# Fewer visits to the turns, another engine for the last copies, and one feature of seven tiles fetched row by row from SyncE

## The chip, the cores and the metric

The kernel runs on one core of one Trainium2 chip. The core has TensorE (PE: matmuls, and "turns", matmuls against an identity that transpose a block), VectorE (DVE), ScalarE (ACT), GpSimd (POOL) and SyncE (SP). Here POOL issues the indirect transfers that gather rows, and SP issues all other transfers. The metric is the device time in microseconds (us) of one execution; the time of a kernel is the median of several. A change is told from no change when it exceeds about 0.2% of the time, some 1.15 us.

## The reference

The kernel is a recommender tower for 2048 samples. Each has 27 ids; id f picks a row of 128 floats from table f. The layer input is the 27 rows side by side (3456 values), the 351 products of each pair of rows, and 16 dense values. Three layers follow.

```python
e = jnp.stack([tbl_0[ids[:, 0]], ..., tbl_26[ids[:, 26]]], axis=1)      # 2048 x 27 x 128
interactions = jnp.einsum('bfd,bgd->bfg', e, e)                          # pair products
flat_interactions = interactions[:, _TRIU_I, _TRIU_J]                    # 351 of them
h = jnp.concatenate([e.reshape(B, -1), flat_interactions, dense_ctx], axis=1)   # 2048 x 3823
h = jnp.maximum(h @ W_top1 + b_top1, 0.0)                                # 512
h = jnp.maximum(h @ W_top2 + b_top2, 0.0)                                # 256
y = h @ W_top3                                                           # 1
```

## The kernel before, in words

The samples are cut into 16 tiles of 128. The 27 features of a tile are cut into 7 groups (`GROUPS`: six of 4 features, the last of 3), called g0 to g6. Feature 23 is the last one of g5. (15, g2) means group 2 of tile 15. Every engine runs its own list of instructions in the order in which the code writes them; semaphores hold them to each other. Nothing is reordered by a scheduler.

For each tile:

- POOL issues one indirect transfer a feature (line 242), each for 128 rows of 512 bytes, into the buffer `emb`, which has one slot a feature. The gather of a feature of tile t waits only until PE has turned that group of tile t-1.
- PE turns each group (`turn_group`, line 269) into one of two banks of `ps_t`. A turn of group n waits for the gathers of the group and for the copy of group n-2.
- ACT rounds the turned group to the "high" part (`split_group`, line 534), then DVE takes what is left as the "low" part (line 645). Both go to `emb_x`.
- PE multiplies each feature by the weights of layer 1 in three matmuls of 512 columns (`multiply`, lines 298 to 300), so a group of 4 has 12 of them.
- PE makes the pair products in 16 "gram units" of two matmuls each (`gram_unit`, line 323), numbered k = 0 to 15, in three banks. ACT copies out the even units and DVE the odd ones (`take_blocks`, lines 582 and 666), four copies a unit. The features whose multiplies are not done yet are spread between the units by the table `BEFORE_UNIT`.
- DVE turns the pair products in blocks (line 680), adds and packs them (lines 687, 702). PE turns the packed columns (`turn_columns`, line 352), ACT copies them, and PE multiplies them (`multiply_columns`, line 356). Then follow the activation, its turn (`turn_h1`, line 393) and layer 2 (`layer_2`, line 400), all one tile late.

In the order of PE a tile looks like this (t > 0): multiply g0, turn g2, multiply g1, turn g3, multiply g2, turn g4, multiply g3, turn the columns, turn g5, multiply two features, multiply the columns, turn g6, then the 16 gram units with the other nine features between them. After unit 8 stand the turns of h1 and of (t+1, g0), after unit 14 those of (t+1, g1), after unit 15 layer 2. A "visit" below is a run of turns with nothing else between; there are seven visits to turns a tile. The last tile has an order of its own, in which the turn of feature 26 (line 286) stands alone and last, since its gather is the last of all.

SP loads the weights of layer 1 in 27 pieces during tile 0, some later weights and constants, and then waits for the last tile to store the output.

## Time and profile before

| | |
|---|---|
| time, median of 3 runs | 574.94 us (574.45 to 575.32) |
| the profiled execution: its time | 576.18 us |
| the profiled execution: its span, first to last instruction | 574.4 us |
| mean granted clock of PE in it | 0.991 |
| busy: PE / its weight loads / DVE / ACT / POOL | 93% / 83% / 60% / 41% / 73% |

The profile shows one execution. Busy shares are averages over the span and say nothing of who waits for whom; PE's matmuls overlap, so 93% is not PE at its peak. The time beside the span, 1.8 us, lies outside the first and last instruction. Starts of rows are in us from the first instruction.

### The profile page before, as it was taken

The page shows a single profiled execution, that of the slowest core. Times are in us where ns is not written, and L with a number is a line of the kernel's source. Part 1 is how long each engine was busy: PE and PEld are TensorE (multiplying, and loading weights), DVE is VectorE, ACT ScalarE, POOL GpSimd, SP SyncE. Part 2 cuts the span into 40 slices and gives each one's busy share as a digit, 9 for nine tenths or more (in the row PEclk, how much of TensorE's full clock was granted, in tenths as well). Part 3 has the DMA queues.
Part 4 walks back from the last instruction along what each step waited for, and adds up shares of the span by engine and source line. Part 5 has one row for each costly group of instructions (what it writes and reads, how often), then busy time and mean ns, then how long its engine had stood idle before and what let it go on. Part 6 is the DMA issues. An engine that isn't in the chain of part 4 may idle for free.

```text
span 574.4 us, 7882 instructions
## 1 busy us (share of the span) xinstructions
PE 535.3 (93%) x2578; PEld 478.4 (83%) x2578; DVE 347.4 (60%) x1140; ACT 233.3 (41%) x703; POOL 417.9 (73%) x450
## 2 busy tenths in 40 slices
PE   0786999999999999999999999999999999999998
PEld 0775988888998888889888898988889888889875
DVE  2756638375583837658373665837467483746754
ACT  3646144351614426262442625335261533517151
POOL 6777777777777777777777777777777777777711
PEclk9989899999999999999999999999999999999999
DMA  7756111211212222121212121212112121212100
GB/s 236 247 161 170 52 53 52 55 51 51 56 51 56 52 55 52 53 54 50 57 51 56 51 55 51 55 53 54 53 51 56 51 57 51 55 51 56 51 15 2
DMA packets 19582, 37.84 MB, mean 66 GB/s; under 512 B 7781, under 2 KB 8805, under 8 KB 19541
## 3 DMA queue, kind: packets, MB, share of 16 engines
q0 software_dynamic: 13824, 28.34, 18.6%
q1 hardware_dynamic: 5716, 8.99, 4.9%
q8 instruction: 21, 0.34, 0.2%
q14 instruction: 21, 0.16, 0.1%
HBM read 37.30 MB, written 0.01 MB: 65 GB/s over the span
## 4 chain that ended last, share of the span: by engine, by line
POOL 69%; issue 22%; PE 6%; DMA 1%; ACT 1%; DVE 0%; ACTq 0%; POOLq 0%; DVEq 0%
POOL emb L242 69%; PE ps_acc L298 1%; PE ps_acc L356 1%; DMA emb<-in_tbl,idx 1%; PE ps_acc L299 1%; PE ps_acc L300 1%; PE ps_gram L323 1%; ACT g_buf L591 0%; PE ps_t L435 0%; PE ps_t L269 0%; DMA idx_first<-in_ids 0%; PE ps_acc L408 0%; PE ps_gram L345 0%; PE ps_t L345 0%; PE ps_t L427 0%
## 5 line engine op out<-in xcount | busy, mean ns | idle before, releaser
L242 POOL DMA_INDIRECT emb<-in_tbl,idx x405 | 386.4, 954 | 123.4 <-issue 121.0
L298 PE MATMUL ps_acc<-w_hi,emb_x 128*128 128x512 f32 x432 | 200.6, 464 | 5.8 <-DVE emb_x L645 5.8
L299 PE MATMUL ps_acc<-w_lo,emb_x 128*128 128x512 f32 x432 | 174.4, 404 | 0.0
L300 PE MATMUL ps_acc<-w_hi,emb_x 128*128 128x512 f32 x432 | 173.4, 401 | 0.0
L645 DVE TENSOR_TENSOR emb_x<-ps_t,emb_x 128x512 fp32r<-128x512 f32 (+1 forms) x111 | 74.1, 667 | 152.5 <-ACT emb_x L534 152.1
L666 DVE COPY g_buf<-ps_gram 32x112 f32<-32x112 f32 x480 | 129.6, 270 | 55.9 <-PE ps_gram L323 49.8
L534 ACT ACTIVATE emb_x<-ps_t 128x512 fp32r<-128x512 f32 (+1 forms) x111 | 63.2, 583 | 223.8 <-PE ps_t L269 223.4
L582 ACT ACTIVATE g_buf<-ps_gram 32x112 f32<-32x112 f32 x480 | 122.6, 255 | 51.9 <-PE ps_gram L323 46.5
L298 PEld LDWEIGHTS ps_acc<-w_hi,emb_x 128*128 128x128 f32 x432 | 131.1, 303 | 11.5 <-issue 8.8
L299 PEld LDWEIGHTS ps_acc<-w_lo,emb_x 128*128 128x128 f32 x432 | 134.5, 311 | 0.6
L300 PEld LDWEIGHTS ps_acc<-w_hi,emb_x 128*128 128x128 f32 x432 | 131.8, 305 | 0.8
L269 PE MATMUL ps_t<-ident,emb 128*128 128x128 f32 x429 | 67.9, 281 | 27.5 <-DMA emb<-in_tbl,idx_first 18.9
L269 PEld LDWEIGHTS ps_t<-ident,emb 128*128 128x128 f32 x429 | 51.8, 143 | 44.9 <-issue 20.7
L323 PEld LDWEIGHTS ps_gram<-emb_x 128*128 128x128 f32 x480 | 69.2, 189 | 11.1 <-ACT g_buf L582 4.2
L323 PE MATMUL ps_gram<-emb_x 128*128 128x224 f32 x480 | 75.3, 285 | 2.1 <-DVE g_buf L666 1.2
L680 DVE STREAM_TRANSPOSE g_buf<-g_buf 128x1792 f32<-128x1792 f32 x16 | 59.0, 3686 | 0.1
L356 PE MATMUL ps_acc<-w_cols,cols_t 128*128 128x512 f32 (+1 forms) x96 | 44.0, 593 | 0.1
L702 DVE TENSOR_TENSOR cols<-gram,g_buf 128x26 f32<-128x26 f32 (+25 forms) x406 | 39.1, 173 | 0.0
L242 POOL DMA_INDIRECT emb<-in_tbl,idx_first x27 | 28.0, 1035 | 9.3 <-issue 7.9
L356 PEld LDWEIGHTS ps_acc<-w_cols,cols_t 128*128 128x128 f32 (+1 forms) x96 | 18.0, 190 | 16.1 <-issue 14.7
L400 PE MATMUL ps_gram<-w,h_t 128*128 128x256 f32 x112 | 26.5, 380 | 0.0
L400 PEld LDWEIGHTS ps_gram<-w,h_t 128*128 128x128 f32 x112 | 20.2, 190 | 2.2
(61 smaller groups left out, 162.8 us busy)
## 6 DMA issues: line engine op xcount, KB each, us to landing
g_buf<-in_W_top SPq DMA_DIRECT2D x27, 256.0 KB, 4.2
emb<-in_tbl,idx POOLq DMA_INDIRECT x405, 2.5
w_cols<-in_W_top SPq DMA_DIRECT2D x1, 512.0 KB
w<-in_W_top SPq DMA_DIRECT2D x1, 512.0 KB
emb<-in_tbl,idx_first POOLq DMA_INDIRECT x27, 3.9
w_cols<-in_W_top SPq DMA_DIRECT2D x1, 222.0 KB
idx<-in_ids SPq DMA_DIRECT2D x1, 216.0 KB, 5.4
ctx_rows<-in_dense_ctx SPq DMA_DIRECT2D x4, 32.0 KB, 5.3
```

The costliest lines, as they stand in the source:

```text
L242: pool.indirect_dma_start(out=emb[:, f * D:(f + 1) * D], out_offset=None, in_=tables[f], in_offset=bass.IndirectOffsetOnAxis(ap=rows, axis ...
L269: last = pe.transpose(turned_bank(n, g)[:, :, i], emb[:, f * D:(f + 1) * D], ident[:, :])
L298: pe.matmul(acc, emb_part(0, f), w_hi[:, f, :], start=(f == 0), stop=False)
L299: pe.matmul(acc, emb_part(0, f), w_lo[:, f, :], start=False, stop=False)
L300: last = pe.matmul(acc, emb_part(1, f), w_hi[:, f, :], start=False, stop=False)
L323: last = pe.matmul(ps_gram[:, n % BANKS, i * NJ * XW:(i + 1) * NJ * XW], gram_weights(q), gram_stream(q), start=True, stop=True)
L356: return pe.matmul(ps_acc[:, t % 2, :], cols_t[0:k, n * P:(n + 1) * P], w_cols[0:k, n, :], start=False, stop=(n == NCC - 1))
L534: act.activation(group_part(0, g), turned_bank(n, g), ACT.Copy).then_inc(s_emb_hi, 1)
L582: last = act.activation(target, source, ACT.Copy)
L645: dve.tensor_tensor(group_part(1, g), turned_bank(n, g), group_part(0, g).bitcast(fp32), ALU.subtract).then_inc(s_emb_lo, 1)
L666: last = dve.tensor_copy(target, source)
L680: dve.transpose(g_turned.rearrange("p n f -> p (n f)"), g_raw.rearrange("p q n -> p n q")).then_inc(s_turned, 1)
```

## The change

There are three parts.

**The order of a tile.** PE turns g2 and g3 in one visit, g4, g5 and the columns in one, g6 alone, and h1, (t+1, g0) and (t+1, g1) in one after unit 11. The table `BEFORE_UNIT` now spreads eleven features instead of nine. ACT and DVE follow: ACT splits (t+1, g0) ahead of its last gram unit, DVE splits it after its last one, the columns are taken after g5, and DVE packs them in one go after g3.

**Who copies the last two gram units.** Unit 14 goes from ACT to DVE and unit 15 from DVE to ACT.

**Feature 23 of tiles 3, 5, 7, 9, 11, 13 and 15.** POOL leaves these seven gathers out. SP loads the ids of these 7 x 128 rows to a small buffer with seven transfers, reads them into registers 32 at a time, and issues one transfer of one row (512 bytes) for each, 896 in all, into a buffer `ahead` of its own that holds all seven tiles. PE's turn of g5 in these tiles waits for the 128 rows as well (`s_ahead`).

```diff
+    ACT_UNITS = [k for k in range(UNITS - 2) if k % 2 == 0] + [UNITS - 1]
+    DVE_UNITS = [k for k in range(UNITS - 2) if k % 2 == 1] + [UNITS - 2]
...
+    AHEAD = 23
+    AHEAD_TILES = [3, 5, 7, 9, 11, 13, 15]
+    LOAD = 32
...
@@ SP, after the weights' loads
+                for n, t in enumerate(AHEAD_TILES):
+                    sp.dma_start(idx_ahead[n:n + 1, :], ids.rearrange(
+                        "(p t) f -> t f p", t=TILES)[t, AHEAD:AHEAD + 1, :]
+                        ).then_inc(s_ids_ahead, 16)
             sp.wait_ge(s_pe_t, NG)
...
+            sp.wait_ge(s_ids_ahead, 16 * NA)
+            for n in range(NA):
+                for p in range(0, P, LOAD):
+                    _, picked = nc.values_load_multi_w_load_instructions(
+                        idx_ahead[n:n + 1, p:p + LOAD], engines=[mybir.EngineType.SP],
...
+                    for i in range(LOAD):
+                        sp.dma_start(ahead[p + i:p + i + 1, n, :],
+                                     tables[AHEAD][bass.ds(picked[i], 1), :]
+                                     ).then_inc(s_ahead[n], 16)
             sp.wait_ge(s_y, TILES)
@@ POOL
                     for f in GROUPS[g]:
+                        if fetched_ahead(t, f):
+                            continue
@@ PE, turn_group
-                pe.wait_ge(s_gather[g], (t + 1) * 16 * len(GROUPS[g]))
+                pe.wait_ge(s_gather[g], gathered(t, g))
+                if AHEAD in GROUPS[g] and t in AHEAD_TILES:
+                    pe.wait_ge(s_ahead[AHEAD_TILES.index(t)], 16 * P)
@@ PE, the tiles
-            BEFORE_UNIT = [2, 0, 0, 2, 0, 0, 2, 0, 0, 1, 0, 0, 2, 0, 0, 0]
+            BEFORE_UNIT = [2, 0, 0, 2, 0, 0, 2, 0, 0, 2, 0, 0, 1, 0, 2, 0]
...
                 turn_group(t, 2)
+                turn_group(t, 3)
                 multiply_group(t, 1)
-                turn_group(t, 3)
                 multiply_group(t, 2)
                 turn_group(t, 4)
-                multiply_group(t, 3)
+                turn_group(t, 5)
                 if t > 0:
                     turn_columns(t - 1)
-                turn_group(t, 5)
-                f = 4 * GF
-                for _ in range(GF if t == 0 else 2):
-                    multiply(t, f)
-                    f += 1
+                multiply_group(t, 3)
                 if t > 0:
                     multiply_columns(t - 1)
                 turn_group(t, 6)
...
-                    if k == 8 and t > 0:
-                        turn_h1(t - 1)
-                    if k in (8, 14):
-                        turn_group(t + 1, (k - 8) // 6)
+                    if k == 11:
+                        if t > 0:
+                            turn_h1(t - 1)
+                        turn_group(t + 1, 0)
+                        turn_group(t + 1, 1)
@@ ACT, the tiles
-                for k in range(0, UNITS, 2):
+                for k in ACT_UNITS:
+                    if k == UNITS - 1:
+                        split_group(t + 1, 0)
                     take_blocks(t, k)
-                    if t > 0 and k == 8:
+                    if t > 0 and k == 10:
                         take_h1(t - 1)
@@ DVE, the tiles
-                for k in range(1, UNITS, 2):
-                    if k == UNITS - 1:
-                        split_group(t + 1, 0)
+                for k in DVE_UNITS:
                     take_blocks(t, k)
+                split_group(t + 1, 0)
                 split_group(t + 1, 1)
```

The rows that follow show how the built programs stand. In the changed program the same helpers have other line numbers: `turn_group` 315, `multiply` 344 to 346, `gram_unit` 369, `turn_columns` 398, `layer_2` 446; the square brackets name the semaphores that a row waits for.

PE before, in the middle of a tile: the end of the multiplies of g3, the columns (352), g5 (269), then features 16 and 17.

```order
L298 MATMUL ps_acc<-w_hi,emb_x 128x512
L299 MATMUL ps_acc<-w_lo,emb_x 128x512
L300 MATMUL ps_acc<-w_hi,emb_x 128x512
L352 MATMUL ps_gram<-ident,cols 128x4x32 [waits s_h2,s_cols]
L352 MATMUL ps_gram<-ident,cols 128x4x32
L352 MATMUL ps_gram<-ident,cols 112x4x32
L269 MATMUL ps_t<-ident,emb 128x128 [waits s_emb_lo,s_gather5]
L269 MATMUL ps_t<-ident,emb 128x128 x3
L298 MATMUL ps_acc<-w_hi,emb_x 128x512 [waits s_emb_lo]
L299 MATMUL ps_acc<-w_lo,emb_x 128x512
L300 MATMUL ps_acc<-w_hi,emb_x 128x512
```

PE in the changed program, the same place: the end of the multiplies of g2, then g4, g5 and the columns in one visit, then the multiplies of g3.

```order
L346 MATMUL ps_acc<-w_hi,emb_x 128x512
L315 MATMUL ps_t<-ident,emb 128x128 [waits s_emb_lo,s_gather4]
L315 MATMUL ps_t<-ident,emb 128x128 x3
L315 MATMUL ps_t<-ident,emb 128x128 [waits s_emb_lo,s_gather5]
L315 MATMUL ps_t<-ident,emb 128x128 x3
L398 MATMUL ps_gram<-ident,cols 128x4x32 [waits s_h2,s_cols]
L398 MATMUL ps_gram<-ident,cols 128x4x32
L398 MATMUL ps_gram<-ident,cols 112x4x32
L344 MATMUL ps_acc<-w_hi,emb_x 128x512 [waits s_emb_lo]
L345 MATMUL ps_acc<-w_lo,emb_x 128x512
L346 MATMUL ps_acc<-w_hi,emb_x 128x512
```

The turn of g5 now stands ahead of the 12 matmuls of g3, and it has one return to multiplies with g4 and the columns instead of two.

PE before, at the end of a tile: unit 14, the turns of (t+1, g1), unit 15, layer 2 (400), and the first multiply of the next tile.

```order
L323 MATMUL ps_gram<-emb_x 128x224 [waits s_dve_raw]
L323 MATMUL ps_gram<-emb_x 128x224
L269 MATMUL ps_t<-ident,emb 128x128 [waits s_emb_lo,s_gather1]
L269 MATMUL ps_t<-ident,emb 128x128 x3
L323 MATMUL ps_gram<-emb_x 128x224 [waits s_act_raw]
L323 MATMUL ps_gram<-emb_x 128x224
L400 MATMUL ps_gram<-w,h_t 128x256 [waits s_h1_out]
L400 MATMUL ps_gram<-w,h_t 128x256 x3
L298 MATMUL ps_acc<-w_hi,emb_x 128x512 [waits s_emb_lo,s_h1]
```

PE in the changed program, the same place: the last multiply ahead of unit 14, units 14 and 15, layer 2, the next tile.

```order
L346 MATMUL ps_acc<-w_hi,emb_x 128x512
L369 MATMUL ps_gram<-emb_x 128x224 [waits s_dve_raw]
L369 MATMUL ps_gram<-emb_x 128x224
L369 MATMUL ps_gram<-emb_x 128x224 [waits s_act_raw]
L369 MATMUL ps_gram<-emb_x 128x224
L446 MATMUL ps_gram<-w,h_t 128x256 [waits s_h1_out]
L446 MATMUL ps_gram<-w,h_t 128x256 x3
L344 MATMUL ps_acc<-w_hi,emb_x 128x512 [waits s_emb_lo,s_h1]
```

The turns of (t+1, g1) no longer stand between units 14 and 15; they went up to the visit after unit 11, and two multiplies stand ahead of unit 14 instead.

SP before, its last rows, then SP in the changed program from the same place on.

```order
L213 DMA ctx_rows<-in_dense_ctx 32x256 x4
L215 DMA b_rows<-in_b_top 128x256
L216 DMA w_rows<-in_W_top 128x256
L220 DMA out<-y 128x16 [waits s_y]
L55 UNCONDITIONAL_BRANCH [waits s_stored]
```

```order
L244 DMA ctx_rows<-in_dense_ctx 32x256 x4
L246 DMA b_rows<-in_b_top 128x256
L247 DMA w_rows<-in_W_top 128x256
L253 TENSOR_LOAD idx_ahead [waits s_ids_ahead]
L258 ISA
L258 DMA ahead<-in_tbl 1x128
L258 ISA
L258 DMA ahead<-in_tbl 1x128
L258 ISA
L258 DMA ahead<-in_tbl 1x128
```

Each row fetched costs SP one register instruction (ISA, it makes the address from the id) and one transfer; a load of 32 ids (TENSOR_LOAD) stands ahead of every 32 rows. The store of the output is now queued behind all 896 rows.

## Rows read from the trace of the kernel before

**Rows 1.** The page: the chain that ended last, by engine.

```profile
POOL 69%; issue 22%; PE 6%; DMA 1%; ACT 1%; DVE 0%; ACTq 0%; POOLq 0%; DVEq 0%
```

**Rows 2.** The page: gathers; count, busy us, mean ns, idle before, its cause.

```profile
L242 POOL DMA_INDIRECT emb<-in_tbl,idx x405 | 386.4, 954 | 123.4 <-issue 121.0
```

**Rows 3.** Timeline of POOL: start, us, instruction, idle before; end of (14, g5), last gather.

```profile
509.36 0.94 POOL L242 DMA_INDIRECT emb<-in_tbl,idx  x1 [0.30 <-issue]
...
547.60 0.94 POOL L242 DMA_INDIRECT emb<-in_tbl,idx  x1 [0.30 <-issue]
```

**Rows 4.** Timeline of PE: the turn of g5 in tiles 1, 2 and 14.

```profile
72.78 0.60 PE L269 MATMUL ps_t<-ident,emb 128*128 128x128 f32 x4
...
105.90 0.60 PE L269 MATMUL ps_t<-ident,emb 128*128 128x128 f32 x4
...
511.85 0.66 PE L269 MATMUL ps_t<-ident,emb 128*128 128x128 f32 x4 [0.49 <-DMA emb<-in_tbl,idx]
```

**Rows 5.** Timeline of PE: from multiplies to a visit and back.

```profile
267.04 0.39 PE L300 MATMUL ps_acc<-w_hi,emb_x 128*128 128x512 f32 x1
267.27 0.60 PE L269 MATMUL ps_t<-ident,emb 128*128 128x128 f32 x4
267.63 0.58 PE L298 MATMUL ps_acc<-w_hi,emb_x 128*128 128x512 f32 x1
268.05 0.40 PE L299 MATMUL ps_acc<-w_lo,emb_x 128*128 128x512 f32 x1
```

**Rows 6.** Timeline of PE: from gram units to multiplies, and the end of a tile.

```profile
248.28 0.52 PE L298 MATMUL ps_acc<-w_hi,emb_x 128*128 128x512 f32 x1
248.64 0.40 PE L299 MATMUL ps_acc<-w_lo,emb_x 128*128 128x512 f32 x1
...
257.65 0.60 PE L269 MATMUL ps_t<-ident,emb 128*128 128x128 f32 x4
258.30 0.49 PE L323 MATMUL ps_gram<-emb_x 128*128 128x224 f32 x2
258.62 1.90 PE L400 MATMUL ps_gram<-w,h_t 128*128 128x256 f32 x8
260.82 0.58 PE L298 MATMUL ps_acc<-w_hi,emb_x 128*128 128x512 f32 x1 [0.30 <-DVE emb_x L645]
```

**Rows 7.** Timeline of DVE: the split of (t+1, g0) and the last copies of a tile.

```profile
259.99 0.69 DVE L645 TENSOR_TENSOR emb_x<-ps_t,emb_x 128x512 fp32r<-128x512 f32 x1 [1.45 <-ACT emb_x L534]
260.59 1.11 DVE L666 COPY g_buf<-ps_gram 32x112 f32<-32x112 f32 x4
```

**Rows 8.** Timeline of PE: turns of tile 15 (g2, g3, g4, columns, g5, 24-25, 26).

```profile
531.48 0.63 PE L269 MATMUL ps_t<-ident,emb 128*128 128x128 f32 x4 [0.31 <-DVE emb_x L645]
...
536.29 0.60 PE L269 MATMUL ps_t<-ident,emb 128*128 128x128 f32 x4
...
541.36 0.66 PE L269 MATMUL ps_t<-ident,emb 128*128 128x128 f32 x4
...
541.96 0.30 PEld L352 LDWEIGHTS ps_gram<-ident,cols 128*128 128x128 f32 x3 [0.19 <-DVE cols L702]
...
546.45 0.65 PE L269 MATMUL ps_t<-ident,emb 128*128 128x128 f32 x4
...
548.98 0.44 PE L279 MATMUL ps_t<-ident,emb 128*128 128x128 f32 x2
550.20 0.33 PE L286 MATMUL ps_t<-ident,emb 128*128 128x128 f32 x1 [0.79 <-DMA emb<-in_tbl,idx]
```

**Rows 9.** Timeline of SP: issues; the first is for a single partition, the last for 128..

```profile
41.81 0.28 SPq L206 DMA_DIRECT2D w_cols<-in_b_top  x1
42.13 0.54 SPq L208 DMA_DIRECT2D w<-in_W_top  x1
...
45.21 0.43 SPq L216 DMA_DIRECT2D w_rows<-in_W_top  x1
```

**Rows 10.** Windows of all engines: busy us, granted clock, DMA share, GB/s.

```profile
240.00:274.00 34.00, 33.12 (x163) 29.84 (x163) 20.80 (x71) 13.74 (x43) 25.77 (x28) 1.00 0.20 53
```

More of the change, by code:

```diff
@@ L73, in dlrm_tower_kernel @@
         emb = sb("emb", [P, NF * D])
+        ahead = sb("ahead", [P, NA, D])
+        idx_ahead = sb("idx_ahead", [NA, P], i32)
         g_buf = sb("g_buf", [P, 2 * Q * XW])
@@ L109, in dlrm_tower_kernel @@
         s_gather_last = sem("s_gather_last")
+        s_ids_ahead = sem("s_ids_ahead")
+        s_ahead = [sem(f"s_ahead{t}") for t in AHEAD_TILES]
         s_zero = sem("s_zero")
@@ L138, in dlrm_tower_kernel, with fetched_ahead, rows_of, gathered @@
         s_stored = sem("s_stored")
+        def fetched_ahead(t, f):
+            return f == AHEAD and t in AHEAD_TILES
+        def rows_of(t, f):
+            if fetched_ahead(t, f):
+                return ahead[:, AHEAD_TILES.index(t), :]
+            return emb[:, f * D:(f + 1) * D]
+        def gathered(t, g):
+            return 16 * sum(1 for u in range(t + 1) for f in GROUPS[g] if not fetched_ahead(u, f))
         def emb_part(part, f):
@@ L198, in _ @@
                                  ids.rearrange("(p t) f -> p (t f)", t=TILES)).then_inc(s_ids, 16)
+            with nc.allow_non_contiguous_dma(reason="one id of every row of ids"):
+                for n, t in enumerate(AHEAD_TILES):
+                    sp.dma_start(idx_ahead[n:n + 1, :], ids.rearrange(
+                        "(p t) f -> t f p", t=TILES)[t, AHEAD:AHEAD + 1, :]
+                        ).then_inc(s_ids_ahead, 16)
             sp.wait_ge(s_pe_t, NG)
@@ L218, in _ @@
                          ).then_inc(s_const, 16)
+            sp.wait_ge(s_ids_ahead, 16 * NA)
[3 more added lines that the diff above has]
+                        idx_ahead[n:n + 1, p:p + LOAD], engines=[mybir.EngineType.SP],
+                        min_val=0, max_val=tables[AHEAD].shape[0] - 1,
+                        skip_runtime_bounds_check_because="an id is a row of its table")
+                    for i in range(LOAD):
+                        sp.dma_start(ahead[p + i:p + i + 1, n, :],
+                                     tables[AHEAD][bass.ds(picked[i], 1), :]
+                                     ).then_inc(s_ahead[n], 16)
             sp.wait_ge(s_y, TILES)
@@ L237, in _ @@
                     for f in GROUPS[g]:
+                        if fetched_ahead(t, f):
+                            continue
                         landed = s_gather[g]
@@ L268, in turn_group @@
                 for i, f in enumerate(GROUPS[g]):
-                    last = pe.transpose(turned_bank(n, g)[:, :, i], emb[:, f * D:(f + 1) * D],
+                    last = pe.transpose(turned_bank(n, g)[:, :, i], rows_of(t, f),
                                         ident[:, :])
@@ L278, in turn_last_group @@
                 for i, f in enumerate(GROUPS[g][:-1]):
-                    last = pe.transpose(turned_bank(n, g)[:, :, i], emb[:, f * D:(f + 1) * D],
+                    last = pe.transpose(turned_bank(n, g)[:, :, i], rows_of(t, f),
                                         ident[:, :])
@@ L466, in _ @@
                 turn_group(t, 6)
+                f = 4 * GF
                 for k in range(UNITS):
@@ L610, in _ @@
                             split_weights(c)
-                    split_group(t, g)
-                    if t > 0 and g == 4:
+                    if t == 0 or g > 0:
+                        split_group(t, g)
+                    if t > 0 and g == 5:
                         take_columns(t - 1)
@@ L615, in _ @@
                         relu_h1(t - 1)
-                for k in range(0, UNITS, 2):
+                for k in ACT_UNITS:
+                    if k == UNITS - 1:
+                        split_group(t + 1, 0)
                     take_blocks(t, k)
-                    if t > 0 and k == 8:
+                    if t > 0 and k == 10:
                         take_h1(t - 1)
             t = TILES - 1
-            for g in range(5):
+            for g in range(1, 5):
                 split_group(t, g)
```

18 lines of the change are left out of this document (7 added, 11 removed).

## The prediction

> **What bounds the kernel now.** Read the chain that ended last first: POOL and "issue" make 91% of it [rows 1]. The group of the gathers says why. A gather keeps POOL 0.95 us, and nearly all the idle time between gathers, 121.0 of 123.4 us, is put down to POOL's own issue and not to another engine [rows 2]. POOL runs gather behind gather, 0.94 + 0.30 = 1.25 us each [rows 3], from the start to the last one at 547.60. Next look at PE where it needs what POOL brings. In tile 14 the turn of g5 waits for its gather and starts 2.49 us after POOL started the last one, 509.36 to 511.85 [rows 3, 4]. In tiles 1 and 2 the same turn waits for nothing, and the distance between them, 105.90 - 72.78 = 33.12 us, is what a tile costs PE alone. From tile 2 to 14 it is (511.85 - 105.90)/12 = 33.83 us, POOL's pace of 27 x 1.25 = 33.75 and a little. So two engines are close: POOL 33.8 and PE 33.1 a tile. A gain on one of them alone is worth at most 0.7 us a tile; the change works on both. PE's clock stays at 2.4 GHz in the steady part (1.00 in the window), and the transfers fill a fifth of the DMA engines [rows 10].
>
> **The gathers left out.** Seven of 1.25 us: POOL ends 8.75 us earlier. Six of them lie ahead of (14, g5). Its data come 7.50 us earlier, and its turn can start at 511.85 - 7.50 = 504.35. POOL needs nothing that the change brings later: the gather of a group waits for the turn of one tile before, which is some 20 us old.
>
> **What the new order saves PE in a tile.** A return from turns to multiplies: from the start of four turns to the second matmul behind them are 268.05 - 267.27 = 0.78 us; four turns at 0.11 (the third and fourth of a waiting group add 0.66 - 0.44 = 0.22 to two, rows 8) and one matmul at 0.24 would be 0.68. So a return costs 0.10 [rows 5]. Two such returns go. The visit between units 14 and 15 costs more: 258.30 - 257.65 = 0.65 for four turns (0.44), and 0.32 for the two matmuls behind it (0.22), together 0.31 [rows 6]; it goes. One more return from gram units to multiplies comes: 0.36 instead of 0.24, so 0.12 [rows 6]. Sum: -0.20 - 0.31 + 0.12 = -0.39. At the start of a tile PE idles 0.30 for DVE's low part of g0 [rows 6, 7]. In the new order DVE copies unit 14 (1.11) and then splits g0 (0.60) behind the unit's matmuls; with about 0.3 to start and 0.15 to be seen, 2.2 us. PE meanwhile has unit 15 and layer 2, some 2.1 (the latter 1.90 busy less its tail). I put 0.1 of the wait as left: -0.20. PE alone then needs 33.12 - 0.39 - 0.20 = 32.5 us a tile. The copies move between ACT and DVE one for one, and both have idle time (13.7 and 20.8 of 34 busy [rows 10]): nothing.
>
> **What sets the pace then.** POOL's pair of tiles takes 2 x 33.83 - 1.25, a mean of 33.2 a tile. PE's 32.5 is below it. So POOL still sets the pace and PE's own saving shows as longer waits at g5, not as time, until tile 14.
>
> **The end.** From (14, g5) on PE has more to do than before, since the turn now stands ahead of the multiplies of g3. Before: 531.48 - 511.85 = 19.63 us to the turn of (15, g2) [rows 4, 8]. Added: 12 matmuls at 0.24 = 2.87 and the three turns of the columns, 0.33. Gone: 0.31 of the visit, 0.20 of the wait for DVE. Back: 0.12. Sum 22.44. From (15, g2) to the last turn, L286, were 550.20 - 531.48 = 18.72, the order of the code there is unchanged, but waits are in it that fall away when gathers come early: 0.95 at L286 (1.22 from the turn of features 24 and 25, which takes 0.27), 0.23 at (15, g4) (5.07 from g3 for four turns and six features that make 4.84), and 0.19 at the columns [rows 8]. Left 17.35. The last turn comes at 504.35 + 22.44 + 17.35 = 544.14. Its gather alone would allow 550.20 - 8.75 = 541.45, so PE sets it: the last tile and a half are PE's. Behind L286 nothing is changed: 574.4 - 550.20 = 24.2. End of the span 568.3, that is 6.1 less. Against the profiled execution's own time, 576.18, that is 570.1; the median of the runs is 1.24 below that execution, so **568.8**.
>
> **SP's rows.** 896 times a register instruction and a transfer, and 28 loads of ids. The trace has no such transfer. Nearest is the one to a single partition, 42.13 - 41.81 = 0.32 from its start to the next; one over 128 partitions lasts 0.43 [rows 9]. For the register instruction I know no row; it should lie between nothing and a whole issue, 0.28. A load of ids for 32 rows costs at most what a gather takes to land, 2.49, so 0.08 a row. Bounds: 0.32 and 0.68 us a row. I take 0.45, near the row for one partition. The loop starts when the last constant is issued, 45.6, and its first ids are there, 48.1. The rows of tile 3 are due at about 138: (138 - 50.6)/128 = 0.68. The last are due at the turn of (15, g5), 544.14 - 3.75 + 0.95 = 541.3: (541.3 - 2.5 - 48.1)/896 = **0.548 us a row**. Below it the rows cost nothing, all under POOL's and PE's time. The edge lies inside my bounds. Behind PE's wait for them stands all of PE's list, and behind that POOL's next gathers; behind SP's rows stands only the store.
>
> The Trainium skill, "DMA: Bandwidth & Descriptors", section "Latency and other measured facts", puts the floor of a tensor load at about 0.6 us; by it the loads would be 0.02 a row instead of 0.08, and the rate 0.4. No row here shows one.
>
> **Rivals.**
> - *SP is too slow.* For: no row for the register instruction, and 896 issues in a row where before there were 40. Against: the single-partition issue, 0.32, leaves 0.23 for the rest. It decides from 0.548 us a row; no gain is left at 0.554. At 0.60 the last rows are issued at 48.1 + 537.6, land 2.5 later, and 574.4 - 546.45 = 28.0 follow: 616.2, median 616.7. Slower.
> - *Rows land one by one.* A one-row transfer may end before the next starts to move. Then a row takes what a gather takes from issue to use, 2.49 [rows 3, 4]: 50.6 + 896 x 2.49 + 28 = 2310 us. Against: gathers start every 1.25 and take 2.49, so they overlap. The page's section "Anatomy of one DMA" has a fixed cost of about 2 us in each, and its rules for kernel authors call small transfers mostly overhead; the trace agrees on the size of it, and shows that it overlaps.
> - *The rows disturb the gathers.* They share DMA engines that are 0.20 busy [rows 10]. If each gather grew by 0.01 us, some 365 of them ahead of (14, g5) shift it by 3.6: 572.5. Against: the rows are 0.46 MB in 490 us, 1 GB/s beside 53. The page's section on a DMA's semaphore says a transfer of few parts uses the lowest-numbered engines; then all rows sit on one engine, with one sixteenth of each gather, which speaks for this rival. No row here shows it.
> - *The long visits make PE wait.* Two groups in a visit need both banks free and DVE's packing done ahead of the columns. If a tile costs PE 33.8, PE sets the pace from tile 1 on: (1, g5) at 72.78 [rows 4] less up to 3 because it stands earlier in the tile, say 71, 13 tiles of 33.8, then 22.44 + 17.35 + 24.2 = 64.0 to the end: 574.4, median 574.9, the same. It starts to cost at 33.2, that is 0.7 us of new waits a tile.
> - *All of POOL's 8.75 show.* If PE loses 2.7 less in the last tile and a half: 566.2.
>
> **How the numbers follow.** Forecast 0.60, with a range of its own of 567.0 to 570.5; SP too slow 0.15; one by one 0.02; disturbed gathers 0.12; long visits 0.06; all of POOL's gain 0.05. Within 0.2% of 574.94 is 573.8 to 576.1, what a measurement can't tell from no change. Faster: 0.60 + 0.05 + 0.10 + 0.02 = 0.77; the same 0.06; slower 0.17. The range, 565.8 to 575.0, takes in all but the two on SP and part of the long visits, about 0.2.
>
> **What would show it.** POOL: 398 gathers by idx, still 1.25 apart, the last one starting near 538.9. PE: waits for gathers at g5 of about 1.5 us in even tiles and a few tenths in odd ones, no wait for a gather at L286; a turn of (15, g2) 5 us earlier than 531.48. SP: rows less than 0.548 apart, done before 541. The forecast is wrong if g5 of odd tiles waits for `ahead`, if the gathers' spacing grows, or if PE's tiles in which it waits for nothing take over 33 us.

## The result, and the profile after

The changed kernel takes 569.41 us, median of 4 runs (568.90 to 569.92); the kernel before 575.13 (574.45 to 575.85, 4 runs, three of them those of the table of before). The ratio is 0.990, interval 0.9883 to 0.9918: faster by 5.7 us, where 6.1 was forecast. The profiled execution took 569.48 and spans 567.6; 568.3 was forecast for the span.

The chain that ended last, from the page, answers to [rows 1]: PE has taken POOL's place as its largest part.

```profile
PE 55%; POOL 29%; issue 10%; DMA 5%; ACT 1%; DVE 1%; ACTq 0%; POOLq 0%; DVEq 0%
```

The group of the gathers (count, busy us, mean ns, idle before, its cause) answers to [rows 2]: seven are gone, the mean of one is what it was.

```profile
L286 POOL DMA_INDIRECT emb<-in_tbl,idx x398 | 379.3, 953 | 121.4 <-issue 116.3
```

POOL's timeline answers to [rows 3]: the last gather of (14, g5), and the last of all, 9.3 us earlier than before.

```profile
501.36 0.95 POOL L286 DMA_INDIRECT emb<-in_tbl,idx  x1 [0.30 <-issue]
...
538.30 0.95 POOL L286 DMA_INDIRECT emb<-in_tbl,idx  x1 [0.30 <-issue]
```

PE's timeline answers to [rows 4, 8]: the visit of g4 and g5 in tiles 2 and 3, then the turns of (14, g5), (15, g2) and the last one, and the first gram pair of the last feature behind it.

```profile
105.63 1.04 PE L315 MATMUL ps_t<-ident,emb 128*128 128x128 f32 x8
...
137.83 0.93 PE L315 MATMUL ps_t<-ident,emb 128*128 128x128 f32 x7
138.59 0.27 PE L315 MATMUL ps_t<-ident,ahead 128*128 128x128 f32 x1
...
503.92 0.66 PE L315 MATMUL ps_t<-ident,emb 128*128 128x128 f32 x4 [1.46 <-DMA emb<-in_tbl,idx]
...
526.03 0.41 PE L315 MATMUL ps_t<-ident,emb 128*128 128x128 f32 x2
...
543.21 0.27 PE L332 MATMUL ps_t<-ident,emb 128*128 128x128 f32 x1
...
544.64 1.15 PE L391 MATMUL ps_gram<-emb_x 128*128 128x224 f32 x8 [0.36 <-DVE emb_x L700]
```

Two tiles without a wait stand 137.83 - 105.63 = 32.2 us apart (33.12 before). From tile 6 on PE waits for gathers at g5 as forecast: 1.4 to 1.7 us in the even tiles, 0.2 to 0.7 in tiles 7, 9 and 11, nothing in 13. At (14, g5) it still waits 1.46. At the last turn it waits for nothing: its gather was started 4.9 us earlier, where 2.5 to 2.6 are needed.

SP answers to [rows 9]. By instruction (duration in ns, min/median/max; first and last start in us): the loads of 32 ids, the transfers of the ids, and the three instructions of a row.

```profile
L253 SPq TENSOR_LOAD <-idx_ahead x28: 2072/2126/2193, 46.2 to 465.1; - x28
L229 SPq DMA_DIRECT2D idx_ahead<-in_ids x7: 592/597/630, 36.8 to 40.7; - x7
```

```profile
L258 SPq FUSED_REGOPS  x896: 37/37/51, 48.3 to 480.0; - x180
L258 SPq MOVE ahead<-in_tbl x896: 29/29/42, 48.4 to 480.0; - x180
L258 SPq DMA_DIRECT2D ahead<-in_tbl x896: 224/225/314, 48.5 to 480.1; - x180
```

The 896 rows take 480.1 - 48.5 = 431.6 us, 0.482 a row. A row without its load is 0.42 of it ((431.6 - 27 x 2.13)/895), the load 0.067. The last row is issued 60 us ahead of its turn.

### The profile page after: what moved, and what is told of

It reads as the page before. It is cut to its first block, busy times and chain, and to the rows that moved or that the text cites. A ratio compares the mean times of both kernels' runs of the same rounds, so it can differ in the third digit from the quotient of the medians.

```text
span 567.6 us, 10600 instructions
## 1 busy us (share of the span) xinstructions
PE 527.5 (93%) x2578; PEld 478.9 (84%) x2578; DVE 348.8 (61%) x1140; ACT 230.5 (41%) x703; POOL 410.7 (72%) x443
## 4 chain that ended last, share of the span: by engine, by line
PE 55%; POOL 29%; issue 10%; DMA 5%; ACT 1%; DVE 1%; ACTq 0%; POOLq 0%; DVEq 0%
POOL emb L286 29%; PE ps_acc L344 12%; PE ps_acc L345 10%; PE ps_acc L346 10%; PE ps_gram L369 6%; PE ps_acc L402 5%; PE ps_t L315 5%; DMA emb<-in_tbl,idx 4%; PE ps_gram L446 2%; PE ps_gram L439 1%; PE ps_gram L398 1%; ACT g_buf L632 0%; PE ps_t L481 0%; PE ps_acc L454 0%; DMA idx_first<-in_ids 0%
## 5 line engine op out<-in xcount | busy, mean ns | idle before, releaser
L286 POOL DMA_INDIRECT emb<-in_tbl,idx x398 | 379.3, 953 | 121.4 <-issue 116.3
L689 DVE TENSOR_TENSOR emb_x<-ps_t,emb_x 128x512 fp32r<-128x512 f32 (+1 forms) x111 | 72.6, 668 | 125.6 <-ACT emb_x L575 124.7
L315 PE MATMUL ps_t<-ident,emb 128*128 128x128 f32 x422 | 62.2, 281 | 34.2 <-DMA emb<-in_tbl,idx_first 21.5
L315 PEld LDWEIGHTS ps_t<-ident,emb 128*128 128x128 f32 x422 | 50.5, 144 | 49.6 <-issue 21.2
L369 PEld LDWEIGHTS ps_gram<-emb_x 128*128 128x128 f32 x480 | 70.4, 192 | 4.3
L369 PE MATMUL ps_gram<-emb_x 128*128 128x224 f32 x480 | 71.2, 280 | 0.0
```

What stands on the lines that cost most here:

```text
L286: pool.indirect_dma_start(out=emb[:, f * D:(f + 1) * D], out_offset=None, in_=tables[f], in_offset=bass.IndirectOffsetOnAxis(ap=rows, axis ...
L315: last = pe.transpose(turned_bank(n, g)[:, :, i], rows_of(t, f), ident[:, :])
L369: last = pe.matmul(ps_gram[:, n % BANKS, i * NJ * XW:(i + 1) * NJ * XW], gram_weights(q), gram_stream(q), start=True, stop=True)
L689: dve.tensor_tensor(group_part(1, g), turned_bank(n, g), group_part(0, g).bitcast(fp32), ALU.subtract).then_inc(s_emb_lo, 1)
```

## The experiments

Each kernel was timed in five rounds beside the kernel before, whose medians in the three sets were 575.19 (e1, e2, e5, e6), 575.32 (e3, e4, e7, e8) and 575.44 us (e9 to e12). The interval is that of the ratio to it; kernels of different sets are best compared by their ratios. "Turn" is the first instruction of the turns named; times inside a run come from its one profiled execution, and executions of one kernel differ by 1 us and more (the spans of e7_split_add: 565.2 to 569.1). A "stretched" gather is one that lasts longer than the 0.945 us of most.

**e1_order_only: the new order and engines, all gathers on POOL.**

```diff
-    AHEAD_TILES = [3, 5, 7, 9, 11, 13, 15]
+    AHEAD_TILES = []
```

> The changed kernel without the rows from SyncE: GpSimd gathers all 432 features, everything else as changed. Theory (GpSimd sets the pace up to tile 14, then TensorE's order): the turn of (14, g5) starts again near 511.8; 22.11 us to (15, g2) and 17.18 to the last turn, as in the changed kernel, make 551.1, and 24.4 to the end: span 575.5, 1.1 us longer than before, ratio about 1.002. Waits for gathers at g5 of about 1.6 us in every tile. Rival (the fewer visits bring the gain): each tile gives 0.4 to 0.9 us, the span is 562 to 569.

Measured: 576.65 us, ratio 1.0023 (1.0009 to 1.0037), span 574.6. The turn of (14, g5) starts at 510.98 behind a wait for its gather, the last turn at 550.27.

```profile
510.98 0.33 PE L316 MATMUL ps_t<-ident,emb 128*128 128x128 f32 x1 [1.47 <-DMA emb<-in_tbl,idx]
...
550.27 0.27 PE L333 MATMUL ps_t<-ident,emb 128*128 128x128 f32 x1
```

As expected: PE's saving of 0.9 us a tile goes into waits of 1.3 to 1.5 us at g5 in tiles 3 to 14, and the way from (14, g5) to the last turn is 39.29 us instead of 38.35 [rows 4, 8]. Alone, the order makes the kernel slightly slower: 1.5 us by the medians, 0.2 by the profiled spans.

**e2_rows_only: the rows from SP, order and engines as before.** The edit to the kernel before is the part of the diff on SP, POOL and `turn_group`.

> The kernel before with the 896 rows from SyncE in place of the same seven gathers, and with its old order of visits and old engines for the copies. Theory: GpSimd brings (14, g5) at 503.9, TensorE alone needs 33.12 us a tile and is at that turn at 105.9 + 12 x 33.12 = 503.3, so it is there in time; then 19.6 to (15, g2) and 17.35 to the last turn make 540.9, and its gather allows 540.8: span 565.3, about 2.3 us shorter than the changed kernel, ratio to before about 0.984. Rival (the new order is needed to turn the saved gathers into time): TensorE's 33.12 with new waits of 0.3 or more a tile, span 569 to 573, longer than the changed kernel.

Measured: 570.57 us, ratio 0.9924 (0.9912 to 0.9937), span 568.5: 3.2 us above the expectation. The turn of (14, g5) starts at 506.80 instead of 503.9. Behind it all went about as expected: the last turn is 37.26 later (36.95 expected).

```profile
506.80 0.44 PE L312 MATMUL ps_t<-ident,emb 128*128 128x128 f32 x2 [0.63 <-DMA emb<-in_tbl,idx]
...
544.06 0.27 PE L329 MATMUL ps_t<-ident,emb 128*128 128x128 f32 x1
```

So POOL was late. Most of its gathers last 0.94 to 0.95, but some last up to 1.53. In e2_rows_only (POOL, then DVE, the same stretches):

```profile
364.76 1.43 POOL L283 DMA_INDIRECT emb<-in_tbl,idx  x1 [0.30 <-issue]
...
502.72 1.15 POOL L283 DMA_INDIRECT emb<-in_tbl,idx  x1 [0.31 <-issue]
```

```profile
364.46 0.92 DVE L730 TENSOR_TENSOR gram<-g_buf 128x729 f32<-128x729 f32 x1
...
502.63 0.42 DVE L760 SCALAR_TENSOR_TENSOR h<-h,w_rows 128x256 f32<-128x256 f32 x1
```

The long gather starts 0.30 behind the start of DVE's add of the pair products, ends at 366.19, and the add ends at 365.38: 0.81 earlier. The second one starts 0.09 into an instruction of layer 3 that also reads two SBUF operands (`h`, `w_rows`), and ends 0.82 after it. The changed kernel has the same thing:

```profile
29.52 1.34 POOL L286 DMA_INDIRECT emb<-in_tbl,idx_first  x1 [0.30 <-issue]
...
165.20 0.94 POOL L286 DMA_INDIRECT emb<-in_tbl,idx  x1 [0.30 <-issue]
166.45 1.48 POOL L286 DMA_INDIRECT emb<-in_tbl,idx  x1 [0.30 <-issue]
```

```profile
29.35 0.69 DVE L682 TENSOR_TENSOR w_lo<-g_buf,w_hi 128x512 fp32r<-128x512 f32 x1
...
165.05 0.64 DVE L689 TENSOR_TENSOR emb_x<-ps_t,emb_x 128x512 fp32r<-128x512 f32 x1
166.21 0.91 DVE L731 TENSOR_TENSOR gram<-g_buf 128x729 f32<-128x729 f32 x1
```

A gather that starts inside the add ends some 0.8 us after the add, so one that starts in the add's last 0.1 us loses nothing; nor does one that has started before it (68.85 against an add at 69.12, 0.95). The other rows are a control: the gather at 29.52 starts inside a subtraction of the same size as DVE's splits, but with both operands in SBUF (`g_buf`, `w_hi`: the low part of the weights, only in tile 0), and is stretched; the one at 165.20 starts inside a split, which has one operand in PSUM (`ps_t`), and is not. In all fourteen traces 480 gathers start inside such a split with at least 0.15 us of it left, and none lasts over 0.95.

So the loss is a matter of phase between POOL's 1.25-us beat and the tile, from nothing to 0.7 us a tile. Against a beat of 1.2485 (the spacing of undisturbed gathers from start to start), the gathers of e2_rows_only lose 8.2 us in all, those of the changed kernel 6.2, those of before 6.7. What they lose up to (14, g5), by the DVE instruction that each stretched gather outlasts by 0.8 us:

| us up to (14, g5) | before | e2_rows_only | changed kernel |
|---|---|---|---|
| the weights' low parts, tile 0 | 2.8 | 2.1 | 2.1 |
| the add of the pair products | 1.1 | 3.6 | 1.8 |
| layer 3's instruction (`h`, `w_rows`) | 1.7 | 1.9 | 0 |

Between the last two kernels that is 3.7 us. The last gather of (14, g5) starts 504.18 - 501.36 = 2.8 us later in e2_rows_only. Most of the 0.9 between the two figures is that the undisturbed gathers of the changed kernel's execution last 947 ns each, those of e2_rows_only 944, for which no run shows a cause. The part of the add became the theory of the next kernels.

**e5_late_g5: in tile 14 alone, PE works before it waits.**

```diff
+                late = t == TILES - 2
+                if late:
+                    multiply_group(t, 3)
                 turn_group(t, 5)
                 if t > 0:
                     turn_columns(t - 1)
-                multiply_group(t, 3)
+                if late:
+                    multiply(t, f)
+                    multiply(t, f + 1)
+                    f += 2
+                else:
+                    multiply_group(t, 3)
```

> The changed kernel, but in tile 14 alone the multiplies of g3 stand ahead of the turn of g5 and the columns, and two features of g4 take their place behind it. Theory: TensorE uses the 1.46 us that it waits there. The turn of (14, g5) starts at 505.2 without a wait, four features fewer lie behind it (22.11 - 2.87 = 19.24 to (15, g2)), then 17.18: 541.7 for the last turn, span 566.1, 1.5 us shorter than the changed kernel. Rival (the last tile and a half are held by something else, the copies or GpSimd): no change, 567.6.

Measured: 568.45 us (567.43 to 569.19, 4 runs), ratio 0.9891 (0.9875 to 0.9907), span 565.6, 0.5 below the expectation. The profiled execution is the fastest of the four; by the ratios the kernel and the changed one (0.990) can't be told apart. In the trace the turn needs no wait, and the last turn is 543.21 - 541.27 = 1.9 earlier than in the changed kernel.

```profile
504.07 0.60 PE L315 MATMUL ps_t<-ident,emb 128*128 128x128 f32 x4
...
541.27 0.27 PE L332 MATMUL ps_t<-ident,emb 128*128 128x128 f32 x1
```

The turn starts 0.15 later than in the changed kernel and has 37.20 us behind it instead of 39.29. So from (14, g5) on it is PE's work, not POOL's gathers, that sets the end.

**e6_old_units: the last two units copied by the old engines, the splits of the next g0 behind them.**

```diff
-    ACT_UNITS = [k for k in range(UNITS - 2) if k % 2 == 0] + [UNITS - 1]
-    DVE_UNITS = [k for k in range(UNITS - 2) if k % 2 == 1] + [UNITS - 2]
+    ACT_UNITS = list(range(0, UNITS, 2))
+    DVE_UNITS = list(range(1, UNITS, 2))
...
@@ ACT, the tiles
                 for k in ACT_UNITS:
-                    if k == UNITS - 1:
-                        split_group(t + 1, 0)
                     take_blocks(t, k)
...
+                split_group(t + 1, 0)
```

> The changed kernel with the old engines for the last two gram units: unit 14 by ScalarE, unit 15 by VectorE, the split of the next g0 behind them. Theory: the low part of g0 is ready some 0.7 us later, so TensorE idles about 0.7 us between layer 2 and the next tile; this is hidden behind the gathers up to tile 14, and only the one at the turn of (15, g2) shows: span 567.6 + 0.6 = 568.2. Rival (the swap brings its wait in every tile): 0.7 x 14 more, 577.

Measured: 571.04 us, ratio 0.9934 (0.9921 to 0.9948). Five of the six runs took 569.59 to 571.98 us and one 2831.64, of which nothing here shows the cause; the ratio leaves it out. The profiled execution is the fastest of them, span 567.8, that of the changed kernel within 0.2. A tile now begins with a wait for DVE, and the wait for the gather at (14, g5) is 0.88 instead of 1.46: the one is paid out of the other.

```profile
459.60 0.58 PE L344 MATMUL ps_acc<-w_hi,emb_x 128*128 128x512 f32 x1 [0.62 <-DVE emb_x L688]
...
503.55 0.66 PE L315 MATMUL ps_t<-ident,emb 128*128 128x128 f32 x4 [0.88 <-DMA emb<-in_tbl,idx]
```

From (14, g5) to the last turn it is 39.8 us instead of 39.3, the 0.6 expected. But the interval lies clear above that of the changed kernel (0.9883 to 0.9918), some 2 us: the old engines cost more than the 0.6, and where the rest arises stays open, since the profiled execution doesn't show it.

**e7_split_add: e2_rows_only with DVE's add in three pieces.**

```diff
-                dve.tensor_tensor(gram[:, :, 0:to], g_turned[:, 0:NF, 0:to],
-                                  g_turned[:, GE:GE + NF, 0:to], ALU.add).then_inc(s_sum, 1)
+                cuts = [0, NF] if t == TILES - 1 else [0, 9, 18, NF]
+                for a, b in zip(cuts, cuts[1:]):
+                    last = dve.tensor_tensor(gram[:, a:b, 0:to], g_turned[:, a:b, 0:to],
+                                             g_turned[:, GE + a:GE + b, 0:to], ALU.add)
+                last.then_inc(s_sum, 1)
```

> The kernel of e2_rows_only (rows from SP, old order and old engines of the last units), with DVE's add of the turned pair products (128x729 in one instruction, 0.91 us) cut into three of nine features each, except in the last tile. Theory 1, gathers on POOL are stretched while this add reads two SBUF operands: a gather then lasts at most some 0.2 us too long where it was up to 0.58; of the 8.2 us of excess over a spacing of 1.2485 some 2.5 to 3 go, the turn of (14, g5) starts at 504.3 instead of 506.8, and the span is 566.0 instead of 568.5. Theory 2, the 3.2 us by which e2_rows_only missed have another cause (random, or the new order itself): the excess and the turn stay, span 568.5 plus or minus 0.3.

Measured: 569.48 us (567.48 to 571.32), ratio 0.9890 (0.9859 to 0.9920); profiled span 567.5, turn of (14, g5) at 505.71, loss over the beat 7.5. That is between the two theories: the add's part is 2.0 us up to (14, g5) instead of 3.6, and the size I gave was wrong, since gathers of up to 1.46 us remain. The interval overlaps that of e2_rows_only. POOL, then DVE:

```profile
162.86 1.35 POOL L283 DMA_INDIRECT emb<-in_tbl,idx  x1 [0.31 <-issue]
```

```profile
162.33 1.06 DVE L732 TENSOR_TENSOR gram<-g_buf 128x243 f32<-128x243 f32 x3
```

The pieces stand back to back, the next starts before the last is over, and this gather ends 0.82 after the end of the third. It gets in between pieces only sometimes.

**e8_late_split: e5_late_g5 with the same cut.**

> The kernel of e5_late_g5 with the same add cut into three. Theory 1 (the add stretches gathers): the 1.6 us or so that its stretched gathers cost between 60 and 500 us shrink to 0.5, the turn of (13, g5) and with it all that follows come about 1.0 earlier, span 564.6. Theory 2 (no such effect, or DVE's longer work delays PE): 565.6 or more.

Measured: 569.29 us (568.16 to 570.39), ratio 0.9886 (0.9861 to 0.9911); profiled span 568.3, loss 6.7 where e5_late_g5 had 4.5. Beside the pieces its gathers lose 2.4 us, beside the whole add in e5_late_g5 2.2. No gain here, so cutting the add is no reliable remedy.

**e9_copy: e2_rows_only with the add's second operand taken away.** Half of the sums is left out.

```diff
-                dve.tensor_tensor(gram[:, :, 0:to], g_turned[:, 0:NF, 0:to],
-                                  g_turned[:, GE:GE + NF, 0:to], ALU.add).then_inc(s_sum, 1)
+                dve.tensor_copy(gram[:, :, 0:to], g_turned[:, 0:NF, 0:to]).then_inc(s_sum, 1)
```

> The kernel of e2_rows_only with DVE's add of the pair products (two SBUF operands) replaced by a copy of its first operand, same shape, same target, one SBUF operand; the second half of the sums is left out. Theory 1, it is the second SBUF operand that stretches POOL's gathers: behind the copy no gather lasts over 1.0 us, the 3.7 us of excess from adds go, the turn of (14, g5) starts at 503.5 instead of 506.8, span 565.3. Theory 2, any long DVE instruction of this shape stretches them: excess and turn stay, 568.5. Theory 3, the copy runs in a faster mode that holds the port as well: its row is near 0.5 us instead of 0.91, stretches of up to 0.35 stay, about 567.

Measured: 565.66 us, ratio 0.9827 (0.9801 to 0.9853), 4.9 less than e2_rows_only; span 564.4. The copy lasts as long as the add did, and a gather that starts 0.06 behind its start keeps its 0.94. POOL, then DVE:

```profile
395.54 0.94 POOL L283 DMA_INDIRECT emb<-in_tbl,idx  x1 [0.30 <-issue]
```

```profile
395.48 0.92 DVE L730 COPY gram<-g_buf 128x729 f32<-128x729 f32 x1
```

The groups of the gathers, of e2_rows_only and of e9_copy:

```profile
L283 POOL DMA_INDIRECT emb<-in_tbl,idx x398 | 381.4, 958 | 121.4 <-issue 119.9 <-PE ps_t L312 1.5
```

```profile
L283 POOL DMA_INDIRECT emb<-in_tbl,idx x398 | 376.9, 947 | 121.4 <-issue 117.1 <-PE ps_t L312 4.3
```

4.5 us of POOL are gone: the 3.6 beside the add, as theory 1 has it, and, since the phase is now another, the 1.9 beside layer 3's instruction, less some that came on elsewhere. All fifteen gathers that start around or inside the copy last 0.94 to 0.95. From tile 2 (105.38) to tile 14 the turns of g5 come 33.1 apart, without waiting for gathers: PE's own pace in the old order. The turn of (14, g5), 502.57, no longer waits, and the last turn is at 540.03. The second SBUF operand is shown as the cause: the copy takes it away at the same length, and the splits above, which are two-operand instructions too but with one in PSUM, rule out that it is the kind of operation. (The packing adds behind it have two in SBUF as well: one gather beside them, at 65.11, still lasts 1.32.)

**e10_double_add: the changed kernel with the add done twice.**

```diff
-                dve.tensor_tensor(gram[:, :, 0:to], g_turned[:, 0:NF, 0:to],
-                                  g_turned[:, GE:GE + NF, 0:to], ALU.add).then_inc(s_sum, 1)
+                for out in [gram] if t == TILES - 1 else [again, gram]:
+                    last = dve.tensor_tensor(out[:, :, 0:to], g_turned[:, 0:NF, 0:to],
+                                             g_turned[:, GE:GE + NF, 0:to], ALU.add)
+                last.then_inc(s_sum, 1)
```

> The changed kernel with DVE's add of the pair products done twice in tiles 0 to 14, the first time into a buffer that nobody reads. DVE has the time (it is busy two thirds). Theory 1: a gather in flight ends 0.80 us after the end of the first or the second add, so that some gathers last 1.8 to 2.3 us and the mean loss grows by 0.4 to 0.85 us a tile: the turn of (14, g5) at 509 to 515 instead of 503.9, span 573 to 578. Theory 2, no coupling of DVE's add and POOL: 567.6 plus or minus 0.3, no gather over 1.5 us but where there was one.

Measured: 570.58 us, ratio 0.9915 (0.9892 to 0.9938), span 568.7. The turn of (14, g5) is at 504.16; no gather lasts over 1.54. The size in my theory failed: the gathers beside the two adds lose 4.0 us in all, against 2.1 beside the one of the changed kernel, 0.1 a tile and not 0.4 to 0.85; less lost elsewhere makes the loss over the beat 6.0 against 6.2. POOL, then DVE:

```profile
365.65 1.31 POOL L287 DMA_INDIRECT emb<-in_tbl,idx  x1 [0.31 <-issue]
367.27 0.94 POOL L287 DMA_INDIRECT emb<-in_tbl,idx  x1 [0.30 <-issue]
```

```profile
365.22 0.92 DVE L733 TENSOR_TENSOR again<-g_buf 128x729 f32<-128x729 f32 x1
366.05 0.92 DVE L733 TENSOR_TENSOR gram<-g_buf 128x729 f32<-128x729 f32 x1
```

The gather ends 0.82 behind the end of the first add, and runs while the second one does, which follows at once. Of the extra 1.1 us of span 0.2 are there at (14, g5), and 0.7 is a wait of PE for the columns in the last tile, packed later.

**e3_row14: the rows of tile 14 in place of those of tile 15.**

```diff
-    AHEAD_TILES = [3, 5, 7, 9, 11, 13, 15]
+    AHEAD_TILES = [3, 5, 7, 9, 11, 13, 14]
```

> The changed kernel with feature 23 of tile 14 fetched by SP in place of that of tile 15. If POOL sets the time of the turn of (14, g5) and PE alone what follows: the turn starts 1.25 earlier, 502.7 instead of 503.9, all that follows too, the last gather starts at the same time as before, span 566.35. PE alone from the turn of (13, g5) at 470.0 could be there at 502.2. If PE had set the pace already, the span stays at 567.6. If POOL's last gather set the end, it stays as well.

Measured: 567.64 us (567.04 to 568.43), ratio 0.9861 (0.9837 to 0.9885), span 566.6: the fastest complete kernel of the study. The turn of (14, g5) starts at 502.94, the last at 542.22, both 1.0 earlier though POOL's last gather starts at 538.19 as before. What POOL delivers after (14, g5) doesn't count; what it delivers ahead of it does. (The last gather ahead of it starts 0.9 earlier, not 1.25: those before it ran 0.3 late against the changed kernel's.)

**e4_eight: eight tiles of rows.**

```diff
-    AHEAD_TILES = [3, 5, 7, 9, 11, 13, 15]
+    AHEAD_TILES = [3, 5, 7, 9, 11, 13, 14, 15]
```

> The changed kernel with eight tiles of rows instead of seven (14 as well as 15). SP's rows of 61.66 us a tile from 48.5 on are issued to the end at 541.8 and landed at 543.8. Theory (SP's pace is an edge, and just beyond it PE waits): the turn of feature 23 in (15, g5), which PE could start at 539.35 + 0.3, starts at 543.8; span 543.8 + 27.0 = 570.8, slower than the changed kernel by some 3 us although POOL has one gather less. If the rows' rate is not what limits, it is 566.35 as for e3_row14.

Measured: 576.40 us (574.56 to 577.09, 12 runs), ratio 1.0014 (1.0000 to 1.0029): the whole gain is gone. SP issues its last row at 543.36, and PE waits (the profile names no releaser, "issue"; the semaphore of the rows is what the code waits for there). PE's timeline, then the windows (us, busy of PE, PEld, DVE, ACT, POOL with counts, granted clock, DMA share, GB/s):

```profile
537.58 1.88 PE L402 MATMUL ps_acc<-w_cols,cols_t 128*128 128x512 f32 x4
544.73 0.87 PE L315 MATMUL ps_t<-ident,emb 128*128 128x128 f32 x3 [5.26 <-issue]
...
546.04 0.63 PE L345 MATMUL ps_acc<-w_lo,emb_x 128*128 128x512 f32 x1
546.47 0.63 PE L346 MATMUL ps_acc<-w_hi,emb_x 128*128 128x512 f32 x1
...
549.95 0.40 PE L345 MATMUL ps_acc<-w_lo,emb_x 128*128 128x512 f32 x1
```

```profile
500.00:538.00 38.00, 37.80 (x186) 34.19 (x186) 23.74 (x94) 14.67 (x46) 29.05 (x30) 1.00 0.21 54
538.00:545.00 7.00, 1.74 (x6) 0.69 (x5) 0.00 (x0) 0.60 (x1) 0.47 (x2) 0.85 0.04 13
545.00:549.00 4.00, 4.00 (x14) 3.32 (x13) 0.69 (x1) 0.60 (x1) 0.00 (x0) 0.50 0.00 0
```

The wait was expected. The turn is 0.9 later than forecast: the last row is issued 1.6 later, 0.9 of it because SP's loop began later (49.45), and PE turns 1.4 behind that issue instead of 2.0. Not expected is what follows: behind 5.3 us of idleness PE runs at half its clock, 1.2 GHz, until about 549.9; a matmul takes 0.43 instead of 0.235, start to start. From this turn to the last one take 4.72 us instead of 543.21 - 540.60 = 2.61, so the wait is paid once more in part: 2.1 of the 3.4 us missing from the expectation (570.8 against 574.2), beside the 0.9. Most of the other 0.4 lies behind the last turn, where the granted clock is 0.97 and 0.95 in two windows (1.00 in the changed kernel).

**e11_both: e3_row14 and e5_late_g5 in one.**

> The two edits that shortened the changed kernel in one: the rows of tile 14 instead of tile 15 (e3_row14) and in tile 14 the multiplies of g3 ahead of the turn of g5 and the columns (e5_late_g5). The turn of (14, g5) is PE's own in e5_late_g5, without a wait, so its data 1.25 us earlier bring nothing: if the pace of PE from the turn of (13, g5) sets the end, the last turn is at 541.3 as in e5_late_g5, span 565.6, median 567.6 plus or minus 0.6. If the two gains add up (1.0 and 2.0), span 564.6.

Measured: 568.24 us, ratio 0.9875 (0.9852 to 0.9898), span 566.6. The gains don't add. PE reaches (14, g5) at 504.87 without a wait, where its data would have allowed 502.2 (the last gather starts at 499.67). The last turn is at 542.16, as in e3_row14 (542.22), and the span is the same, 566.6: PE arrives at the turn 1.9 later and has 2.0 less behind it. Once the data are early, turning late brings nothing.

**e12_load16: ids read 16 at a time.**

```diff
-    LOAD = 32
+    LOAD = 16
```

> The changed kernel with the ids read into registers 16 at a time instead of 32, so 56 loads instead of 28. A load of 32 ids takes 2.13 us in the changed kernel's trace. If that price is per load: 70.6 us for the 128 rows of a tile, 0.552 a row; the rows land some 0.5 late for tile 11, 4 late for the turns of g5 in tiles 13 and 15; PE waits there, span 571 to 572. If it is per id: a load takes 1.1 us, the rate stays 0.48 a row, and the span stays 567.6. If between (a floor of 0.6 and the rest per id): 1.35 a load, 0.502 a row, span 567.6 too.

Measured: 570.22 us, ratio 0.9906 (0.9882 to 0.9929), span 568.7. The loads:

```profile
L253 SPq TENSOR_LOAD <-idx_ahead x56: 1134/1232/1402, 47.8 to 485.9; - x56
```

16 ids 1.23 us, 32 ids 2.13: 0.056 an id and 0.34 a load. 0.497 a row, between the two pure cases; no turn of g5 waits for rows. The extra 1.1 us of span are already there at (14, g5), 504.98, where PE waits for a gather: up to there POOL's gathers lose 6.6 over the beat instead of 5.5, and 0.7 of the difference lies in the first 60 us, beside the low parts of the weights.

## Why the prediction was right

*POOL sets the pace until (14, g5).* Right: forecast 504.35, measured 503.92. e1_order_only and e3_row14 show it from two sides: with PE's saving alone nothing is gained; one more gather taken away ahead of (14, g5) brings 1.0, though the last gather of all starts when it did. It isn't the pace in every tile: in tiles 5 and 13 PE waits for no gather.

*PE alone needs 32.5 a tile.* 32.2. The sum of small terms held; the wait of 0.1 that I left at the tile's start isn't there, and the other 0.2 is not traced.

*From (14, g5) to the end PE sets the time.* Right, as e5_late_g5 shows. Forecast 22.44 and 17.35, measured 22.11 and 17.18; the tail 24.4 instead of 24.2, since PE waits 0.36 for DVE's split of the last feature. The four differences, -0.43, -0.33, -0.17 and +0.2, make the 0.7 by which the span came out shorter. The median is nevertheless 0.6 above the forecast: I took 1.24 off the profiled execution of before, and the one of after lay at its median. That correction was the largest error: the span came out 0.7 short and the median 0.6 over.

*SP's rows: 0.45 a row.* 0.482, below the edge of 0.548. The row's three instructions cost 0.42 (I had no row for the register instructions) and the load nearly what I bounded, 0.067 a row against 0.08. The rival "SP is too slow" was the right one to fear: e4_eight, with one tile of rows more, crosses the edge and loses all. The Trainium skill, "DMA: Bandwidth & Descriptors", section "Latency and other measured facts", has 0.6 us as a floor; the loads here, 1.23 and 2.13, grow with the ids, and by the floor alone the load's share would have been little over a quarter of what it is.

*Rows land one by one; rows disturb the gathers.* Both rivals are out: the rows keep up at 0.48, and a gather takes 953 ns on average, 954 before. The undisturbed ones take 944 ns in e2_rows_only, with the same rows, and 944 before.

*Two parts, one gain.* Alone the order gives +1.5 us against 575.19 and the rows -4.6; together -5.7 against their own 575.13. The order and the engines are worth 1.1 then, which the intervals (0.9912 to 0.9937 and 0.9883 to 0.9918) hardly tell from nothing, and this is not PE's saving of 0.9 a tile, which shows as waits at g5. In the traces the turn of (14, g5) comes 2.9 earlier than in e2_rows_only because POOL's gathers meet DVE's instructions in a better phase, and the new order then gives 2.0 back: 39.29 us to the last turn instead of 37.26. Most of the gain, 4.6 us, is the seven gathers. With the new order and the old engines, e6_old_units, the ratio is that of the rows alone, 0.9934 against 0.9924.

*What the prediction didn't have.* It read POOL's pace as 27 x 1.25 "and a little". The little is gathers held by DVE's two-operand instructions, some 6 us up to (14, g5), half of them in tile 0. I had taken them over from the trace of before without seeing them. That came out right for the changed kernel by luck: it loses 5.5 us there where before lost 5.9, but in other places, more beside the add and nothing beside layer 3. In e2_rows_only it loses 8.2, hence the one large miss of the first set. Without the add's second operand (e9_copy, which leaves out half of the sums) the old order and the rows make a kernel that PE sets from tile 2 on, 4.9 us below e2_rows_only by the medians: that is what the coupling of the add, with the phase that it brings, costs there.

The Trainium skill, "SBUF — State Buffer", section "Who interferes with whom", states that a DVE instruction with two SBUF inputs contends with a GpSimd instruction that reads SBUF, and that this is an exclusive lock in which the later of the two is blocked. The traces agree for one direction: an add of 0.92 us holds a gather that starts in it, and the copy of 0.92 us holds none. They don't show the other: an add that starts while a gather is under way, at whatever point of it, starts right behind the instruction ahead of it and lasts as long as ever (0.88 to 0.95 us in the eleven traces with the undivided or doubled add). The same section has it, as inferred, that such an add doesn't delay POOL's transfers, since making descriptors needs the write side. Here it does delay the gathers' issue on POOL; the indirect gather may be held where it reads its ids from SBUF, which no run here separates.

## What to carry to other kernels

Where two engines are within 3% of each other, a saving on one becomes waiting on the other: work out the pace with both, and look for the last point at which the slower one is waited for; behind it only the other's work counts. Here the last such point was (14, g5). A few expensive issues can be moved to an idle queue at a price per row, if the rate is known: measure it at once, since just beyond the edge the loss is larger than the gain. And look at the longest of a group's instructions, not only at its mean: gathers of 1.5 us among those of 0.95 pointed to another engine's instruction.

## What the runs showed of the hardware

- An indirect gather (0.945 us on POOL) that starts while DVE adds two SBUF operands ends 0.81 to 0.83 after the add (a start in the add's last 0.1 us changes nothing): up to 1.53 us in the changed kernel, 1.67 in e12_load16. The same beside a subtraction of the weights (128x512, both operands in SBUF, 1.34 at 29.52 in the changed kernel) and layer 3's instruction (1.15 in e2_rows_only). With one operand in PSUM, or a copy of the same length, nothing. The add itself isn't delayed by a gather under way.
- Back-to-back adds of 0.92 us let a gather in after the first (e10_double_add), pieces of 0.3 not always (e7_split_add).
- A one-row transfer with its address in a register costs SP 0.42 us with its register instructions; loading ids 0.34 a load and 0.056 an id (e12_load16).
- In e4_eight, behind 5.3 us without work, PE ran at 1.2 GHz instead of 2.4 for the next 5 us (granted clock 0.50 from 545 to 549).
